# A graph network's convolutions as matmuls over a dense adjacency that is built first

## The chip, the cores and the metric

The program runs on one core of one Trainium2 chip. The metric is the device time of one execution in microseconds; lower is better. The kernel before took 4636.26 us (median of three runs, 4625.92 to 4641.4).

## What is computed

A graph has 3125 nodes with 256 features each and 103125 directed edges, sorted by their target. Two blocks follow one another: two graph convolutions (GCN), then two attention layers (GATv2). Each block adds its input and normalises every row. Only the first block is touched by the change, and one by-product of it that the second needs.

```python
def gcn_conv(x, src, dst, ew, W, b):          # twice, with a leaky ReLU (0.01) between
    h = x @ W                                 # 3125 x 256
    # self-loops of weight 1 are appended to src, dst and ew
    deg = segment_sum(ew, dst)                # per node
    dis = where(deg > 0, rsqrt(deg), 0)
    norm = dis[src] * ew * dis[dst]
    return segment_sum(h[src] * norm[:, None], dst) + b
x = layernorm(x + gcn_conv(leaky(gcn_conv(x, W1, b1)), W2, b2))
x = layernorm(x + gat2(elu(gat1(x))))         # 4 heads of 64, then 1 head of 256
```

## The kernel before

All tensors are fp32 but the transposed one-hots. The nodes are cut into 25 windows (`NWIN`) of 125 (`WN`). The edges, in the order of their targets, are cut into 806 tiles (`NT`) of 128; four tiles are a block (`NB` = 202 blocks). A block can reach over the border of two windows, so the work items are 228 pieces (`NG`), one for each pair of block and window, with tables that the kernel makes itself from the edge list (`codes`: block and window of each piece, read into registers).

The program is a row of stages, each its own block of instructions on all engines, with a barrier between: `consts`, `route` (edge list in, turned to edge-on-partition columns `dst_t`, `src_t`, `w_t`), `degrees` (the degrees, `dis`, and x @ W1 scaled by `dis` into `acc`, which it also stores to `table_d[0]`), `gcn_edges(0)`, `gcn_mid`, `gcn_edges(1)`, `gat_in(1)`, `gat_edges(1)`, `gat_in(2)`, `gat_edges(2)`, `finish`.

`gcn_edges(layer)` sums the weighted neighbours of one convolution. GpSimd gathers the source rows, one indirect DMA for each of the 806 tiles of 128 rows (`gather_blocks`, L1009), into a ring of 16 blocks `rows`. For each piece VectorE makes four weighted one-hots `selw` (L1146, 128 edges x 128 nodes), TensorE multiplies the four with the gathered rows (L1185, fp32, 256 columns) and VectorE adds the result to the window's rows of `acc` (L1157). In layer 0 the same loops also make what the attention layers need later: four bf16 one-hots `ohk` of each piece (L1164), turned by TensorE (L1193), copied from PSUM by ScalarE (L1215) and widened to fp32 (L1220), and stored from ScalarE's queue to `oh_d` and `ohT_d` (256 KB and 128 KB a piece). Some flags for the attention's segments (`marks`) are made at its start on VectorE.

`gcn_mid` applies bias, leaky ReLU and W2 window by window, and stores the rows to `table_d[1]`.

The attention stages use the same gather (806 indirect DMAs each), load the stored one-hots, and are not changed by the diff but for an index into the list of tables.

The order on each engine is the order of the code: `pipeline` unrolls 12 pieces, with a lag in pieces for each step, in a loop of 19 turns. Engines are bound by semaphores alone: GpSimd runs ahead in the ring until the pieces that free a slot are summed (`s_mm`), TensorE waits for a landed block (`s_landed`) and for its one-hots (`s_sel`).

Of the kernel before, what the change touches and what calls it, by code (L numbers as in the profile page):

```python
# [12 lines left out]
P = 128  # L13
N_NODES = 3125
N_EDGES = 103125
D = 256
# [30 lines left out]
META = 4  # L47
BIG = 1.0e30
# [147 lines left out]
def gnn_kernel(nc, a, out):  # L196
    ctx = ExitStack()
    with ctx:
# [18 lines left out]
        def close(st):  # L217
# [8 lines left out]
            with nc.Block() as block:  # L226
                @block.gpsimd
                def _(pool):
# [13 lines left out]
        table_d = [nc.dram_tensor(f"table{i}_d", (N_NODES, w), F32, kind="Internal").ap()  # L242
                   for i, w in enumerate((D, D, DX, DX))]
# [33 lines left out]
        natf_dst = sb("natf_dst", [P, NTJ, P], F32, marked)  # L277
        nat_w = sb("nat_w", [P, NTJ, P], F32, marked)
# [5 lines left out]
        same = sb("same", [P, NTJ, P], F32, marked)  # L284
        flg_all = sb("flg_all", [P, NTJ, 5, P], F32, marked)
        ends_all = sb("ends_all", [P, 2, NTJ], F32, marked)
        linesT = sb("linesT", [2 * NTJ, P], F32, marked)
        bidx = sb("bidx", [HG, 2], U32, marked)
        apart = sb("apart", [HG, 2, 2], F32, marked)
        link4 = sb("link4", [HG, 2, K], F32, marked)  # L290
        alone4 = sb("alone4", [HG, 2, K], F32, marked)
        into = sb("into", [NC, CH * K], F32, marked)
        alone_at = sb("alone_at", [NC, 2, CH * K], F32, marked)
        through = sb("through", [NC, 2, CH * K], F32, marked)
        carry_all = sb("carry_all", [NC, 4, CH * K], F32, marked)


        found = ExitStack()
        tri = sb("tri", [P, P], F32, found)
# [24 lines left out]
        def route():  # L324
# [5 lines left out]
            natf_src = sb("natf_src", [P, NTJ, P], F32, st)  # L330
# [315 lines left out]
        def one_hot(tile, w, b):  # L646

            return nc.vector.tensor_tensor(tile, nodes_of(w).unsqueeze(1).to_broadcast([P, K, P]),
                                           dst_t[:, bass.ds(b, 1), :].rearrange("p o k -> p (o k)").unsqueeze(2).to_broadcast([P, K, P]),
                                           ALU.is_equal)  # L650

        def degrees():
# [56 lines left out]
            s_W, s_mm, s_h, s_d, s_in, s_deg_all, s_root, s_dis, s_sc, s_set = (sem(n) for n in (  # L709
# [14 lines left out]
            with nc.Block() as block:  # L724
# [27 lines left out]
                def _(sp):  # L752
# [10 lines left out]
                    for v in range(TURNS):  # L763
                        if v == TURNS - 2:
                            sp.wait_ge(s_sc1, 1)
                        else:
                            sp.wait_ge(s_sc, v + 1 if v < TURNS - 2 else v)
# [141 lines left out]
                def _(act):  # L909
# [33 lines left out]
                    for v in range(*PARTS[0]):  # L943
                        scale(v, s_sc)
# [1440 lines left out]
```

## Time and profile before

| | us |
|---|---|
| median of 3 runs (range) | 4636.26 (4625.92 to 4641.4) |
| span of the profiled execution | 5635.5 |
| of it: `consts`, `route`, `degrees` | 0 to 104 |
| `gcn_edges(0)`, `gcn_mid`, `gcn_edges(1)` | 104 to 2552 |
| attention layer 1 (its edges 2690 to 4100) | 2552 to 4100 |
| attention layer 2 (its edges 4230 to 5570) | 4100 to 5570 |
| `finish` | 5570 to 5635.5 |

The profiled execution is 999 us longer than the median of the runs; no other time of it was taken, so its span stands for it. Times in rows below are from its start. An instruction's duration includes a fixed latency that the next one can overlap, so the spacing of starts is shorter than the mean duration. "Busy" is the union of such durations. An fp32 matmul stands in the trace as two TensorE instructions, each with its own weight load.

### The profile page before, as it was taken

The numbers are of one execution on the slowest core, as the hardware profiler recorded it, in microseconds if no ns is written. First come the engines' busy times: TensorE is split into PE (matmuls) and PEld (weight loads), VectorE is DVE, ScalarE is ACT, GpSimd is POOL, SyncE is SP. The second block draws the span as 40 slices with busy tenths as digits, with TensorE's granted clock in tenths as the row PEclk, the third lists the DMA queues.
The fourth block names the chain that finished last, engine by engine and source line by source line (L and its number), as shares of the span: only waits on it lengthen the run. The fifth ranks groups of instructions, "written<-read, shape, count | busy, mean of one in ns | idle before, by whom it ended". The sixth has DMA issues, their size and how long they took to land. (4 is left out here: it accounts for less than half of the span.)

```text
span 5635.5 us, 95010 instructions
## 1 busy us (share of the span) xinstructions
PE 3517.4 (62%) x15636; PEld 2585.4 (46%) x15637; DVE 3007.8 (53%) x9011; ACT 1856.5 (33%) x6057; POOL 3154.3 (56%) x3421
## 2 busy tenths in 40 slices
PE   4555555555555554556577676776755777777776
PEld 3344444444333333333455555555534555555554
DVE  5444444444322222225677777777765665665655
ACT  3222222122000000003476767666732333333334
POOL 4666666664666666661555555555325555555550
PEclk7777777777667777778788888888987888888887
DMA  4555555554323233334556556555535666665665
GB/s 138 159 168 160 162 159 167 156 167 125 89 87 91 87 90 89 89 89 104 149 172 172 171 168 177 172 170 165 148 83 150 176 171 168 175 172 168 179 172 136
DMA packets 469883, 816.01 MB, mean 145 GB/s; under 512 B 86378, under 2 KB 271484, under 8 KB 469692
## 3 DMA queue, kind: packets, MB, share of 16 engines
q0 software_dynamic: 156464, 429.23, 27.7%
q1 hardware_dynamic: 245866, 294.48, 17.6%
q10 hardware_dynamic: 67362, 90.53, 4.4%
q14 instruction: 167, 1.37, 0.1%
q8 instruction: 24, 0.39, 0.0%
HBM read 640.50 MB, written 173.40 MB: 144 GB/s over the span
## 5 line engine op out<-in xcount | busy, mean ns | idle before, releaser
L1009 POOL DMA_INDIRECT rows<-table_d,idx x3224 | 3068.0, 952 | 1981.3 <-issue 970.2
L1185 PE MATMUL psum<-rows,selw 128*128 x3648 | 1247.6, 499 | 1085.0 <-issue 416.1
L1185 PEld LDWEIGHTS psum<-rows,selw 128*128 128x128 f32 x3648 | 868.5, 251 | 1383.2 <-issue 1244.1
L2097 ACT ACTIVATE px<-rows,px 128x64 f32 (+1 forms) x4480 | 1280.6, 367 | 205.7 <-issue 140.5
L2162 PE MATMUL psum<-px,ohf 128*128 128x264 f32 (+1 forms) x3648 | 1141.4, 467 | 150.9 <-ACT px L2097 66.5
L1929 DVE TENSOR_TENSOR m<-rows,psum 128x1024 f32<-128x1024 f32 x456 | 554.3, 1216 | 878.3 <-remote 582.8
L2162 PEld LDWEIGHTS psum<-px,ohf 128*128 128x128 f32 x3648 | 801.7, 231 | 334.7 <-issue 99.4
L2113 PE MATMUL psum<-xr,ohT 125*128 x5472 | 780.5, 298 | 143.2 <-issue 54.8
L1157 DVE TENSOR_TENSOR acc<-acc,psum 125x256 f32 x456 | 189.7, 416 | 1239.3 <-DMA nat_w<-in_edge_weight_dram 431.2
L2113 PEld LDWEIGHTS psum<-xr,ohT 125*128 125x128 bf16 x5472 | 578.0, 107 | 336.2 <-issue 185.7
L1146 DVE TENSOR_SCALAR selw<-iotaw,dst_t,w_t 128x128 f32 x1824 | 528.8, 360 | 278.1 <-issue 273.0
L1653 ACT ACTIVATE root<-mv 125x5 f32<-125x5 f32 x5 | 1.1, 213 | 1217.6 <-DVE mv L1410 1217.6
L1215 ACT COPY ohTk<-psum 128x512 bf16<-128x512 bf16 x228 | 132.7, 582 | 641.5 <-remote 526.7
L2088 ACT COPY px<-pl 128x32 f32<-128x32 f32 (+1 forms) x456 | 100.2, 220 | 699.4 <-PE psum L2162 267.8
L1948 DVE SCALAR_TENSOR_TENSOR sc<-m,psum 128x256 f32<-128x256 f32 x912 | 324.2, 403 | 2.9 <-issue 2.8
L1957 DVE TENSOR_REDUCE lg<-sc 128x16 f32<-128x1024 f32 x228 | 278.1, 1220 | 10.3
L1941 DVE SCALAR_TENSOR_TENSOR sc<-m,psum 128x1024 f32<-128x1024 f32 x228 | 273.7, 1201 | 4.2 <-issue 4.1
L1220 ACT CAST ohfk<-ohk 128x512 f32<-128x512 bf16 x228 | 140.8, 618 | 318.6 <-issue 148.2
L1164 DVE TENSOR_SCALAR ohk<-iotaw,dst_t 128x128 bf16 x912 | 211.1, 309 | 21.4 <-issue 21.3
L2062 DVE SCALAR_TENSOR_TENSOR part<-part,keep_tab,psum 128x264 f32<-128x264 f32 (+1 forms) x380 | 180.2, 474 | 17.0 <-PE psum L2162 16.8
L2075 ACT ACTIVATE both<-both 96x128 f32<-96x128 f32 (+1 forms) x76 | 23.4, 308 | 424.7 <-DVE fac L2022 308.1
L2123 PE MATMUL psum<-ident,lg 128*96 128x128 f32 (+1 forms) x152 | 36.5, 328 | 134.4 <-issue 64.1
(321 smaller groups left out, 2052.9 us busy)
## 6 DMA issues: line engine op xcount, KB each, us to landing
ohf<-oh_d SPq DMA_DIRECT2D x456, 256.0 KB
oh_d<-ohfk ACTq DMA_DIRECT2D x228, 256.0 KB
ohT<-ohT_d SPq DMA_DIRECT2D x456, 128.0 KB
rows<-table_d,idx POOLq DMA_INDIRECT x3224
part_d<-part SPq DMA_DIRECT2D x228, 132.0 KB
part_d<-part SPq DMA_DIRECT2D x228, 129.0 KB
ohT_d<-ohTk ACTq DMA_DIRECT2D x228, 128.0 KB
flg<-flags_d SPq DMA_DIRECT2D x228, 40.0 KB
```

Source lines behind the costliest of these rows:

```text
L1009: pool.indirect_dma_start(out=rows[0:n, s % RING, k, :], out_offset=None, in_=table, in_offset=bass.IndirectOffsetOnAxis(ap=idx[0:n, s // ...
L1146: last = nc.vector.tensor_scalar(sel[:, g.pos % DEEP, k, :], nodes_of(w), dst_t[:, bass.ds(b, 1), k:k + 1].rearrange("p o k -> p (o k)"), ...
L1157: nc.vector.tensor_tensor(sums, sums, ps[g.pos % DEEP][0:WN], ALU.add).then_inc(s_acc, 1)
L1164: last = nc.vector.tensor_scalar(ohb[:, g.slot, k, :], nodes_of(w), dst_t[:, bass.ds(b, 1), k:k + 1].rearrange("p o k -> p (o k)"), None, ...
L1185: last = nc.tensor.matmul(ps[g.pos % DEEP], sel[:, g.pos % DEEP, k, :], rows[:, bass.ds(r, 1), k, :].squeeze(1), start=k == 0, stop=k == K ...
L1929: V.tensor_tensor(m[:, i], rows[:, bass.ds(r, 1), :, 0:D].squeeze(1), psX[i], ALU.add).then_inc(s_add, 1)
L1941: V.scalar_tensor_tensor(out=sc[:, i], in0=m[:, i], scalar=0.0, in1=psatt.unsqueeze(1).to_broadcast([P, K, D]), op0=ALU.max, op1=ALU.mult) ...
L1948: last = V.scalar_tensor_tensor(out=sc[:, i, k], in0=m[:, i, k], scalar=0.0, in1=psatt, op0=ALU.max, op1=ALU.mult, accum_out=lg[:, g.half, ...
L1957: V.tensor_reduce(out=kh(lg[:, g.half, g.place]), in_=sc[:, g.slot % 2].rearrange("p k (h c) -> p (k h) c", h=H), axis=AX.X, op=ALU.add).t ...
L2097: last = nc.scalar.activation(px[:, i, k, h, 0:C], rows[:, bass.ds(r, 1), k, h * C:(h + 1) * C].squeeze(1), ACT.Copy, scale=px[:, i, k, h, ...
L2113: last = nc.tensor.matmul(psX[i][:, k, :], ohT[0:WN, g.slot, k * P:(k + 1) * P], xr3[0:WN, bass.ds(w, 1), j, :].squeeze(1), start=j == 0, ...
L2162: last = nc.tensor.matmul(psA[i], ohf[:, g.pos % FS, k, :], px[:, i, k].rearrange("p h c -> p (h c)"), start=k == 0, stop=k == K - 1)
```

## The change

The three GCN stages go, and with them `table_d[0]`, the first table of gathered rows, and the stores to it at the end of `degrees`. In their place stand three stages.

`parts` works out, from the edge list in its natural layout (`natf_dst`, `natf_src`, `nat_w`: a tile of 128 edges on one partition), a second cut: targets in groups of 5 nodes (`GN`, 625 groups), and one part for each pair of tile and group that it touches, 1440 parts in all (`NP`, the rest empty). For each part it puts the tile's columns, rows and weights on partitions with one-hot matmuls (168 bf16 matmuls of 480 columns, L1206), exactly, as sums of two or three bf16 pieces: `col_at`, `row_at`, `w_at`. It also makes `slots` (a PSUM column for each part) and `units`.

`adjacency` builds, for each window of 125 targets, the dense matrix of edge weights against all 3125 sources. Each part is one fp32 matmul of 125 by 125 (L1329): the stationary operand `sw` is one-hot in the source's row in its window times the weight, the moving operand `where` is one-hot in (target in the group, source's window). The sum goes to a register-held column of PSUM, over what other parts have put there. 16 parts are a step, 90 steps. GpSimd makes ten of a step's `where` one by one (L1281), VectorE the other six in one instruction (L1258) and all 16 `sw` (L1294). ScalarE copies finished units of PSUM (20 targets by 25 source windows, 500 columns) to a strip and zeroes them. SP stores each of the 25 strips (125 x 3125 fp32) to `adj_d`.

`convolve` runs both layers: 50 products, one for each layer and window, each 25 fp32 matmuls of 256 columns (L1630) with the strip (`adj_w`, three in flight) stationary and the feature rows moving. The self-loop, bias, ReLU and W2 of a finished window run beside the next one. The 228 pieces' one-hots for the attention layers, and the flags, are made in the same loops, five pieces to a product, and are now stored from SP's queue. No row is gathered before the attention layers. In the diff below the loops of `adjacency` are those of GpSimd, VectorE, ScalarE and TensorE in this order, those of `convolve` are SP's and TensorE's.

```diff
-            rows = sb("rows", [P, RING, K, D], F32, st)
-            sel = sb("selw", [P, DEEP, K, P], F32, st)
-                    gather_blocks(pool, table_d[layer], idx, rows, s_idx, s_rows, s_mm, s_landed, s_mm, 6)
-                        for k in range(K):
-                            last = nc.tensor.matmul(ps[g.pos % DEEP], sel[:, g.pos % DEEP, k, :], rows[:, bass.ds(r, 1), k, :].squeeze(1),
-                                                    start=k == 0, stop=k == K - 1)
...
+        def parts():
...
+                    for j in range(NTJ):
+                        if j >= 2:
+                            dve.wait_ge(s_tiles, j - 1)
+                        link(V.tensor_scalar(tmp[j % 2][:], iotaw[:, 0:NP], begin[:, j:j + 1], None, ALU.is_ge))
+                        V.scalar_tensor_tensor(out=of_tile[:, j], in0=iotaw[:, 0:NP], scalar=end[:, j:j + 1], in1=tmp[j % 2][:],
+                                               op0=ALU.is_lt, op1=ALU.mult).then_inc(s_tiles, 1)
...
+                    gather((0, 1, 2), (offb[:, 0], offb[:, 1]), s_heads)
+                    gather((3, 4, 5), (colb[0], colb[1]), s_atcol)
+                    gather((6, 7, 0), (srb,), s_atrow)
+                    gather((1, 2, 3), (wb[0], wb[1], wb[2]), s_atw)
...
+        def adjacency():
...
+                    for s in range(NS):
+                        if s >= DEEP:
+                            pool.wait_ge(s_mm, STEP * (s - DEEP + 1))
+                        for i in range(POOLED):
+                            p = s * STEP + i
+                            last = nc.gpsimd.tensor_scalar(where[:, s % DEEP, i, :], aim[:], col_at[:, p:p + 1], None, ALU.is_equal)
...
+                        place(s, POOLED, STEP).then_inc(s_where, 1)
+                        for i in range(STEP):
+                            last = V.tensor_scalar(sw[:, s % DEEP, i, :], iota[:, 0:WN + 1], row_at[:, p:p + 1], w_at[:, p:p + 1],
+                                                   ALU.is_equal, ALU.mult)
...
+                            nc.scalar.copy(strip[0:WN, w % 2, :, nodes_at(i)],
+                                           sums_of(u).rearrange("p (d s) -> p s d", s=NWIN)).then_inc(s_strip, 1)
+                            nc.scalar.copy(sums_of(u), zero[0:WN, 0:sums_of(u).shape[1]]).then_inc(s_free, 1)
...
+                        for i in range(STEP):
+                            nc.tensor.matmul(flat[0:WN, bass.ds(at_slot[i], MC)], sw[:, g.slot, i, 0:WN], where[:, g.slot, i, :],
+                                             start=False, stop=True, skip_group_check=True).then_inc(s_mm, 1)
...
+        def convolve():
...
+                    for n in range(CONVS):
+                        for k in pieces_in(n):
+                            store(k)
+                        if n + RA < CONVS:
+                            load(n + RA)
...
+                        for s in range(NWIN):
+                            last = nc.tensor.matmul(psC[n % 2], adj_w[0:WN, n % RA, s, :], rows[0:WN, s, 0:D],
+                                                    start=s == 0, stop=s == NWIN - 1)
+                            if s % PER == PER - 1 and s // PER < len(ks):
+                                turn(ks[s // PER])
+                            if s == 8 and 0 < n <= NWIN:
+                                turn_rows(n - 1)
+                            if s == 18 and 0 < n <= NWIN:
+                                weigh(n - 1)
```

On TensorE, a turn of the loop of `gcn_edges(0)` in the kernel before reads (one piece; `selw` are the weighted one-hots, `rows` the gathered rows, `ohk` the one-hots for the attention):

```order
L192 ISA
L1185 REGISTER_ALU
L1185 ISA
L1185 MATMUL psum<-rows,selw 128x256
L1185 ISA
L1185 MATMUL psum<-rows,selw 128x256
L1185 ISA
L1185 MATMUL psum<-rows,selw 128x256
L1185 ISA
L1185 MATMUL psum<-rows,selw 128x256
L1193 MATMUL psum<-identb,ohk 128x128 x4
```

Each piece had a wait for its landed block (L192) and four products with gathered rows. In the changed kernel the same engine, inside one product of `convolve`, reads (`adj_w` is a strip of the adjacency, `acc` the feature rows, `aT` the turned rows of the window before):

```order
L1630 MATMUL psum<-acc,adj_w 125x256 x5
L1588 MATMUL psum<-identb,ohk 128x128 x4
L1630 MATMUL psum<-acc,adj_w 125x256 x4
L1596 MATMUL psum<-ident,act_in 128x125 x2
L1630 MATMUL psum<-acc,adj_w 125x256
L1588 MATMUL psum<-identb,ohk 128x128 x4
L1630 MATMUL psum<-acc,adj_w 125x256 x5
```

The products now come in fives with nothing between that a gather has to release. On VectorE the loop of `adjacency` reads (two steps of 16 parts):

```order
L1258 TENSOR_TENSOR where<-aim,col_at 128x750 [waits adj_summed]
L1294 TENSOR_SCALAR sw<-iota,row_at,w_at 128x126 x16
L1258 TENSOR_TENSOR where<-aim,col_at 128x750 [waits adj_summed]
L1294 TENSOR_SCALAR sw<-iota,row_at,w_at 128x126 x16
```

and on GpSimd beside it:

```order
L1281 TENSOR_SCALAR where<-aim,col_at 128x125 [waits adj_summed]
L1281 TENSOR_SCALAR where<-aim,col_at 128x125 x9
L1281 TENSOR_SCALAR where<-aim,col_at 128x125 [waits adj_summed]
L1281 TENSOR_SCALAR where<-aim,col_at 128x125 x9
```

Both engines work on the same step at the same time, with addresses that are fixed in the code.

## Rows read from the trace of the kernel before

**Rows 1.** The page: busy us of each engine (share) and instructions.
```profile
PE 3517.4 (62%) x15636; PEld 2585.4 (46%) x15637; DVE 3007.8 (53%) x9011; ACT 1856.5 (33%) x6057; POOL 3154.3 (56%) x3421
```

**Rows 2.** Windows by stage: us, busy of PE, PEld, DVE, ACT, POOL, PEclk, DMA share, GB/s.
```profile
104.00:1350.00 1246.00, 723.73 (x2889) 538.85 (x2890) 555.08 (x2123) 277.95 (x502) 787.65 (x842) 0.75 0.52 161
1362.00:2552.00 1190.00, 608.45 (x1824) 436.54 (x1824) 342.21 (x1140) 0.00 (x0) 771.67 (x830) 0.73 0.31 90
2690.00:4100.00 1410.00, 982.37 (x5047) 736.36 (x5044) 1039.24 (x1868) 957.95 (x3910) 743.54 (x804) 0.85 0.58 166
4230.00:5570.00 1340.00, 983.98 (x5056) 739.32 (x5056) 807.15 (x3220) 449.04 (x1254) 746.88 (x806) 0.83 0.60 168
```

**Rows 3.** Timeline of GpSimd in the second convolution: start, us, what.
```profile
1802.54 0.95 POOL L1009 DMA_INDIRECT rows<-table_d,idx  x1 [0.30 <-issue]
1804.80 0.94 POOL L1009 DMA_INDIRECT rows<-table_d,idx  x1 [1.32 <-issue]
```

**Rows 4.** GpSimd's waits, 1362 to 2552: us in total, times, longest.
```profile
POOL rows L1009 <- issue: 288.9, 768, 4.2
POOL rows L1009 <- DMA nat_w<-in_edge_weight_dram: 100.9, 29, 6.3
```

**Rows 5.** GpSimd's waits in the first attention layer, 2690 to 4100.
```profile
POOL rows L1009 <- remote: 197.0, 80, 3.4
POOL rows L1009 <- issue: 196.7, 631, 1.0
POOL rows L1009 <- PE psum L2113: 187.3, 57, 8.4
```

**Rows 6.** TensorE's timeline: start, us, an fp32 matmul of 256 columns.
```profile
5606.42 1.06 PE L2238 MATMUL psum<-own_rows,with_row 125*125 125x256 f32 x2
5607.28 0.91 PE L2236 MATMUL psum<-x1s,with_row 126*125 126x256 f32 x2
...
5609.33 0.60 PE L2236 MATMUL psum<-x1s,with_row 126*125 126x256 f32 x2
5609.76 0.60 PE L2238 MATMUL psum<-own_rows,with_row 125*125 125x256 f32 x2
```

**Rows 7.** TensorE's timeline, first attention input: fp32 matmuls of four columns.
```profile
2602.96 0.50 PE L1764 MATMUL psum<-watt,yT 128*125 128x4 f32 x4
```

**Rows 8.** Windows as in rows 2: a dense fp32 stretch of that stage.
```profile
2580.00:2600.00 20.00, 18.62 (x77) 10.41 (x75) 9.27 (x19) 14.36 (x39) 0.00 (x0) 1.00 0.23 65
```

**Rows 9.** The weighted one-hots on VectorE: durations in ns, min/median/max.
```profile
L1146 DVE TENSOR_SCALAR selw<-iotaw,dst_t,w_t x1824: 327/341/603, 114.6 to 2545.1; 128x128 f32 x183
```

**Rows 10.** Timeline of VectorE and GpSimd in `degrees`.
```profile
25.53 0.22 DVE L879 COPY from_first<-ident 128x128 f32<-128x128 f32 x1
25.66 0.22 DVE L880 COPY from_last<-ident 128x128 f32<-128x128 f32 x1
...
76.35 2.74 POOL L748 IOTA iotaw<- 128x3128 f32 x1
76.57 0.17 DVE L864 SCALAR_TENSOR_TENSOR deg<-deg,deg_last 128x15 f32<-128x15 f32 x1
76.78 2.34 DVE L865 TENSOR_SCALAR degpos<-deg 128x15 f32<-128x15 f32 x1
```

**Rows 11.** Groups of instructions, 0 to 100: busy us, mean ns, idle before.
```profile
L884 DVE TENSOR_TENSOR is_last<-dst_t,psum 128x808 f32<-128x808 f32 x1 | 1.0, 997 | 0.1
L730 POOL TENSOR_TENSOR w_other<-other,nat_w 128x896 f32<-128x896 f32 x1 | 2.1, 2113 | 1.6 <-DVE other L881 1.6
```

**Rows 12.** TensorE turns one piece's bf16 one-hots, in layer 0's timeline.
```profile
607.91 0.39 PE L1193 MATMUL psum<-identb,ohk 128*128 128x128 bf16 x4
```

**Rows 13.** A group of the page, on ScalarE, busy us and mean ns.
```profile
L1220 ACT CAST ohfk<-ohk 128x512 f32<-128x512 bf16 x228 | 140.8, 618 | 318.6 <-issue 148.2
```

**Rows 14.** Windows as in rows 2: loads of 2.5 KB rows, loads of 1 KB rows.
```profile
38.00:40.00 2.00, 2.00 (x4) 0.84 (x3) 1.92 (x8) 0.16 (x2) 1.55 (x2) 0.50 1.02 385
...
2556.00:2560.00 4.00, 0.00 (x0) 0.00 (x0) 1.17 (x1) 0.00 (x0) 0.00 (x0) 0.55 1.08 190
```

More of the change, by code:

```diff
@@ L47 @@
 META = 4
+GN = 5
+GROUPS_ALL = N_NODES // GN
+STEP = 16
+NS = -(-(NT + GROUPS_ALL) // (3 * STEP)) * 3
+NP = NS * STEP
+THIRD = NP // 3
+BANKS = 8
+UG = 4
+WG = WN // GN
+UW = -(-WG // UG)
+UNITS = NWIN * UW
+MC = GN * NWIN
+POOLED = 10
+CENTRE = 89375
+CONVS = 2 * NWIN
+RA = 3
+OSL = 6
+PER = 5
 BIG = 1.0e30
@@ new lines, in parts @@
+            colb = [sb("colb", [P, NTJ, P], BF16, st) for _ in range(2)]
+            col_r = sb("col_r", [P, NTJ, P], F32, st)
+            wb = [sb("wb", [P, NTJ, P], BF16, st) for _ in range(3)]
+            w_r = [sb("w_r", [P, NTJ, P], F32, st) for _ in range(2)]
+            tmp = [sb("from_begin", [P, NP], BF16, st) for _ in range(2)]
+            of_tile = sb("of_tile", [P, NTJ, NP], BF16, st)
+            below = sb("below_unit", [P, 3, THIRD], BF16, st)
+            limit = sb("limit", [P, 2], F32, st)
@@ L1070, in gcn_edges @@
             LINES = 16 * 7
+            AHEAD = 2
+            pieces_in = lambda n: range(min(n * PER, NG), min((n + 1) * PER, NG))
+            window_in = lambda n: n % NWIN
             with nc.Block() as block:
@@ new lines, in _ @@
+                    for n in range(RA):
+                        load(n)
+                    sp.dma_start(W[:, :, 0:D], a["L0_gnn_W2"].rearrange("(h p) d -> p h d", p=P)).then_inc(s_W, 16)
+                    bcast_row(sp, b, a["L0_gnn_b1"], s_W)
+                    line = lambda v: v.rearrange("(o e) -> o e", o=1)
+                    sp.dma_start(link_d[0:1, 0:1], none[:, 0:1]).then_inc(s_lines, 16)
+                    sp.dma_start(line(in_line(link_d)[TILES + 1:TILES + K]), none[:, 0:K - 1]).then_inc(s_lines, 16)
@@ L1107, in _ @@
                     DVE = mybir.EngineType.DVE
+                    V = nc.vector
                     def marks():
[L1110 removed]
                         done = [0]
@@ L2350, in gnn_kernel @@
         degrees()
-        gcn_edges(0)
-        gcn_mid()
-        gcn_edges(1)
+        adj = ExitStack()
+        col_at, row_at, w_at = (sb(n, [P, NP], F32, adj) for n in ("col_at", "row_at", "w_at"))
+        slots = sb("slots", [1, NP], I32, adj)
+        units = sb("units", [1, NS], I32, adj)
+        unit_ends = sb("unit_ends", [1, UNITS], I32, adj)
+        parts()
+        adjacency()
+        adj.close()
+        convolve()
         marked.close()
```

712 lines of the change are left out of this document (466 added, 246 removed).

## The prediction

> **What bounds the kernel now.** I read the page's totals first, then the windows by stage, then one engine's waits in each. The totals [rows 1] show no engine over 62% of the span, so the bound has to be sought stage by stage. In both convolutions [rows 2] GpSimd is the busiest engine after TensorE (788 of 1246 us, 772 of 1190), and TensorE's busy time stands at a mean granted clock of 0.75 and 0.73, a mix of its two levels, which tells of bursts and pauses. GpSimd's timeline shows that its pauses are not free time: an indirect DMA of 0.95 us is followed by 0.30 us in which nothing is waited for, and each fourth by 1.32 us [rows 3]. Over the second convolution it waits 289 us for "issue", and 101 us for the largest other release [rows 4]. So the gather's own instructions pace the convolutions: 806 of them in 1190 us, 1.48 us each, of which 1.25 is the instruction and its issue. In the attention stages GpSimd waits 397 us of 1410 for others [rows 5], VectorE is busy for 1039 and TensorE for 982 [rows 2]: there the gather is one of several limits.
>
> **Profile and runs.** The sum is made against the profiled execution, span 5635.5 us; the runs' median is 4636.26, 999 us less. That gap has to be put somewhere. TensorE's rows double exactly when its clock halves (below), so they hold nothing that the profiler adds; I put it into the indirect DMAs, of which there are 4 x 806 = 3224. If they cost x less each in an unprofiled run, the two convolutions (bound by them) win 1612x, the attention layers a part a of 1612x. With a = 1, x is 0.31 us and the attention's part 500 us; with a = 0.4, 285 us. As GpSimd waited for others 397 of 1410 us, I take a = 0.6: x = 0.39 us, 375 us in attention and 624 in the convolutions. So in a run the convolutions of the kernel before take about 2448 - 624 = 1824 us. The attention stages stay as they are, and keep their 375.
>
> **The change, part by part**, in profiled time. The three stages that go stand from 104 to 2552.
>
> *`degrees`*: its last vector work ends at 96, the table's stores land by 104 and go. About -6 us; it ends at 98.
>
> *`parts`*, new: VectorE makes `of_tile` in 7 pairs of 1440 columns. By the 808-column row of 997 ns [rows 11], 1.2 ns a column, a two-input one takes 1.7 us and the one-input one 1.0 at its double rate: 19 us. Ten 896-column operations are some 11 us, thirty small links at 0.2 us 6, the chain on `group` 14. The 168 matmuls of 480 columns take 0.2 us at the full clock and 0.4 at the half: 34 to 67 us, of which the first half waits for `of_tile`. On the path: 32 before the matmuls, then some 48 of them and copies. 80 us (65 to 110).
>
> *`adjacency`*, new, 90 steps of 16 parts, each engine three steps deep, so the slowest engine of a step sets it.
> - VectorE: an `sw` is like `selw`, median 341 ns [rows 9]. Two copies of 220 ns started 130 ns apart [rows 10], so the spacing is 90 ns under the duration: 0.25 us. 16 x 0.25 = 4.0; the 750-column `where` 0.85 to 0.9, by its columns [rows 11]. 4.9 us.
> - TensorE: an fp32 matmul of 256 columns at full clock takes 0.434 us (5609.76 less 5609.33), at the half clock 0.86 (5607.28 less 5606.42), with new weights for each and the load hidden [rows 6]. 125 columns are half of that, 0.21. Loads alone, four with 4-column matmuls in 0.50 us, are 0.1 us apart [rows 7], the same as half a matmul of 125 columns, so a load can just hide. 16 x 0.21 = 3.4 us; with nothing hidden, or at the half clock, 6.7.
> - GpSimd: no one-input row of that size. Its iota wrote 3128 columns in 2.74 us, 0.875 ns each [rows 10]; its two-input product took 2.36 ns a column [rows 11]. For 125 columns that is 0.11 to 0.30 us, plus a start. Ten are 2 to 4 us: hidden behind VectorE by themselves.
> - The two together: while the iota ran, VectorE's two-input operation took 0.17 us, but its one-input TENSOR_SCALAR of 15 columns took 2.34 us and ended with the iota [rows 10]. `sw` is such a one-input TENSOR_SCALAR, and GpSimd now runs beside all of them. Low end: nothing is held, 4.9 us. High end: all is in line, 4.9 + 3.0 = 7.9. I take the part of each GpSimd operation in which it moves its columns as held, 10 x 0.11 = 1.1: 6.0 us. That is nearest to the iota's row, whose whole length was columns.
>
> The Trainium skill ("GPSIMD Engine Reference", 1. Specifications) says that GpSimd's SBUF interfaces are shared with VectorE, and that they contend with a two-port mode or with two SBUF inputs. The trace agrees for the first (2.34 us) and not for the second (0.17 us, with two inputs). By the rule `where` on VectorE would be held too, which with all in line is the 7.9 us again, not more.
>
> ScalarE has 175 units of a copy and a zeroing, 0.6 us each [rows 13], with a register load and a wait between: some 2.2 us of the 3.1 that a unit lasts. Hidden; its cover ends under 4.3 us a step. SP's strips, 25 of 1.56 MB, are 5 us each at 350 GB/s [rows 14], once in 21 us. Hidden but for the last, with the last unit 15 us. 90 x 6.0 + 15 + 5 at the start = 560 us (460 to 730).
>
> *`convolve`*, new. On TensorE 1250 + 50 fp32 matmuls of 256 columns x 0.434 = 564; 228 turns of four, four in 0.39 us of which some 0.2 is latency that the next one overlaps [rows 12]; between that and 0.39, near the low end, 0.24 each, 55 (89 at the high); 50 turned blocks of feature rows 12: 631 us, and 18 for joins between kinds. The stretch at 2580 to 2600 shows the clock at 1.00 with TensorE busy 18.6 of 20 us in fp32 [rows 8]; here it is as dense, so full clock. VectorE: 912 `ohk` at 0.25 at most, by `selw`, 228 us, and 40 for the windows' ends. ScalarE: 456 copies at 0.6 [rows 13], 270. Both hidden. What waits on the path: the start, where the first matmul waits for the first strips and then for W2 queued behind three of them, 4.7 MB at 350 GB/s, 14 us and latencies, while the flags are made: 18. The end 3. In all 670 us (640 to 780).
>
> *Transfers*: 50 strips are 78 MB and the one-hots' stores 90 MB, 168 MB in 670 us, 251 GB/s. The trace has 385 GB/s at a share of 1.02 with 2.5 KB runs and 190 at 1.08 with 1 KB runs [rows 14]; the strips have 12.5 KB runs, the stores 2 and 1 KB. At 350 for strips and 2 KB and 190 for 1 KB: 223 + 171 + 158 = 552 us. Hidden, with little to spare.
>
> *Sum*: 98 + 80 + 560 + 670, and 5 for the barriers, is 1413 where 2552 stood: the span falls by 1139 to 4496. The attention's 375 us less in a run: 4121. From the other side, 4636 - 1824 + (1413 - 104) = 4121. I say 4120.
>
> **The rivals.**
> - *VectorE and GpSimd in line.* The 2.34 us row speaks for it, the short hold of a 125-column operation against. 90 x 1.9 = 171 more: 4290.
> - *Transfers bound `convolve`.* If all 168 MB go at the 190 GB/s of 1 KB runs, it takes 883 us, 213 more: 4330. For it: stores and loads mixed never passed 180 GB/s in a long stretch, 161 to 168 [rows 2]. Against: there the share was 0.52 to 0.60.
> - *Better than I think.* Steps at 4.9 us (-99) and the attention's part of the gap 500 us (-125): 3896, say 3900. For it: GpSimd's columns cost little; a could be 1.
> - *Slower: TensorE stays at the half clock.* Place: `convolve` and `adjacency`, which TensorE carries. At 1.2 GHz the fp32 matmuls cost 0.86 us, `convolve` +580 us, a step at least 6.7, +75, `parts` +30: 4805. It decides from +516 us on, that is when `convolve` runs below about 0.6 of full clock. For it: 0.73 to 0.75 in the convolutions now [rows 2]. Against: those have pauses, and rows 8 is dense and at 1.00.
>
> **Chances.** Forecast 0.50, better 0.18, in line 0.15, transfers 0.12, slower 0.05. The range takes in the bounds of both doubtful terms, the hold and the gap: 3880 to 4340. A difference under 0.3% (14 us) can't be told from none. Faster 0.95, same 0.01, slower 0.04 (in a fifth of the half-clock cases it falls short of +516).
>
> **What would show it.** Right: no DMA_INDIRECT before the attention but `degrees`' 25 and the flags' four; a span near 4500 that is some 375 above the run's time; L1329 in groups of 16 every 6 us; L1630 at 0.434 us start to start at a granted clock near 1. Hold: L1294 longer than 341 ns while L1281 runs. Wrong: L1630 waiting for `adj_w`'s DMA (transfers), a clock near 0.5, L1329 in one dense row (then TensorE sets the step, not VectorE), or a gap between span and run that stays at 999 or vanishes, which would put it elsewhere than into the gathers.

## The result and the profile after

The changed kernel takes 3845.48 us (median of 4 runs, 3841.91 to 3846.22), the kernel before 4634.13 (median of 4, 4625.92 to 4641.4): a ratio of 0.830, 95% interval 0.829 to 0.831. The profiled execution took 3845.3 us with a span of 3843.6, so the gap of 999 us between span and runs that stood in front of the prediction is gone. The prediction said 4120 (3880 to 4340): the direction was right and the new stages together came out as forecast; the total was 275 us too high, and the measured time lies 35 us under the range. Of the times below, one run of experiment 2 (4519 us at a granted clock of 0.78, where its other three took 4416 to 4435 at 0.86) was in a slow state and is left out of its ratio.

The page, as in [rows 1]:

```profile
PE 2980.3 (78%) x17564; PEld 2375.2 (62%) x17565; DVE 2904.3 (76%) x8382; ACT 2023.3 (53%) x6416; POOL 2197.2 (57%) x2660
```

The windows by stage, with the columns of [rows 2]: `parts`, `adjacency`, `convolve`, then a stretch in each attention layer and everything behind the convolutions.

```profile
98.00:154.00 56.00, 36.90 (x172) 17.04 (x172) 42.89 (x40) 6.53 (x7) 0.30 (x1) 0.81 0.00 0
154.00:766.00 612.00, 400.04 (x2909) 380.82 (x2909) 501.58 (x1545) 189.35 (x350) 583.16 (x904) 0.88 0.29 69
781.00:1414.00 633.00, 632.11 (x3562) 536.15 (x3562) 245.62 (x1018) 267.95 (x506) 8.93 (x10) 1.00 0.92 262
1560.00:2560.00 1000.00, 789.18 (x4764) 610.23 (x4762) 961.41 (x1743) 890.25 (x3713) 742.88 (x794) 0.98 0.78 225
...
2700.00:3760.00 1060.00, 855.62 (x5072) 658.92 (x5072) 824.92 (x3257) 450.18 (x1245) 773.05 (x837) 0.93 0.78 216
...
1414.00:3843.60 2429.60, 1866.66 (x10764) 1411.79 (x10764) 2045.21 (x5564) 1513.88 (x5450) 1570.39 (x1682) 0.93 0.73 204
```

GpSimd is now the full engine in `adjacency` (583 of 612 us), TensorE in `convolve` (632 of 633, at a clock of 1.00). The convolutions end at 1413, where the prediction's sum says 1413. The attention, which the diff does not touch, went through 794 GpSimd instructions (nearly all gathers) in 1000 us where [rows 2] has 804 in 1410, at 225 GB/s in place of 166. That is where the missing 275 us lie.

The lines that carry the new stages: durations in ns as min/median/max, then first and last start.

```profile
L1281 POOL TENSOR_SCALAR where<-aim,col_at x900: 590/597/1382, 154.5 to 736.4; 128x125 f32<-128x125 f32 x180
L1258 DVE TENSOR_TENSOR where<-aim,col_at x90: 924/940/1164, 154.5 to 723.6; 128x750 f32<-128x750 f32 x90
L1294 DVE TENSOR_SCALAR sw<-iota,row_at,w_at x1440: 331/337/441, 155.3 to 728.7; 128x126 f32<-128x126 f32 x180
L1329 PE MATMUL psum<-where,sw x2880: 270/272/569, 162.1 to 740.8; 128*125 128x125 f32 x192
L1630 PE MATMUL psum<-acc,adj_w x1250: 377/379/792, 781.0 to 1112.9; 125*125 125x256 f32 x179
L1630 PE MATMUL psum<-second,adj_w x1250: 377/379/433, 1113.3 to 1412.7; 125*125 125x256 f32 x179
```

Two steps on VectorE and part of one on GpSimd, from the timeline (start, us, what, how many, and in brackets the idle time before):

```profile
409.75 1.16 DVE L1258 TENSOR_TENSOR where<-aim,col_at 128x750 f32<-128x750 f32 x1 [3.91 <-PE psum L1329]
410.83 4.68 DVE L1294 TENSOR_SCALAR sw<-iota,row_at,w_at 128x126 f32<-128x126 f32 x16
415.44 0.92 DVE L1258 TENSOR_TENSOR where<-aim,col_at 128x750 f32<-128x750 f32 x1
416.29 4.62 DVE L1294 TENSOR_SCALAR sw<-iota,row_at,w_at 128x126 f32<-128x126 f32 x16
420.83 0.93 DVE L1258 TENSOR_TENSOR where<-aim,col_at 128x750 f32<-128x750 f32 x1
```

```profile
405.72 4.06 POOL L1281 TENSOR_SCALAR where<-aim,col_at 128x125 f32<-128x125 f32 x7
```

VectorE needs 5.39 us for a step (415.44 to 420.83) and after some steps waits (3.91 us before 409.75); GpSimd never waits: 900 in 582 us, 6.47 us for ten. Seven that stand alone in the second timeline start 0.58 us apart ((4.06 less 0.596) / 6). The one that starts with VectorE's `where` at 400.3 is the odd one, and those while VectorE has nothing at all to do (406 to 409.7) are like the rest:

```profile
L1281 POOL TENSOR_SCALAR where<-aim,col_at x1: 1363/1363/1363, 400.3 to 400.3; 128x125 f32<-128x125 f32 x1
...
L1281 POOL TENSOR_SCALAR where<-aim,col_at x7: 593/596/597, 405.7 to 409.2; 128x125 f32<-128x125 f32 x7
```

So ten cost 10 x 0.58, and 0.7 for the one that VectorE's two-input instruction holds. The Trainium skill ("GPSIMD Engine Reference", 1. Specifications) says that GpSimd's interfaces to SBUF are shared with VectorE, and contend with it in a two-port mode or with two SBUF inputs. For two inputs the trace agrees: 1363 ns beside the two-input `where`, 0.59 us beside the one-input `sw`. Which mode `sw` runs in no trace shows.

VectorE is held too, though the median of 337 ns hides it. The group's mean on the page is 364 ns, and in a stretch of the changed kernel with GpSimd busy throughout, ten `sw` have a median of 365 and a maximum of 404:

```profile
L1294 DVE TENSOR_SCALAR sw<-iota,row_at,w_at 128x126 f32<-128x126 f32 x1440 | 417.9, 364 | 0.0
...
L1294 DVE TENSOR_SCALAR sw<-iota,row_at,w_at x10: 334/365/404, 278.6 to 281.3; 128x126 f32<-128x126 f32 x10
```

The last step of experiment 3 (below) has 16 `sw` with GpSimd done. They take 4.17 us together, where the same 16 take 4.62 to 4.68 in the timeline above:

```profile
732.25 0.94 DVE L1258 TENSOR_TENSOR where<-aim,col_at 128x750 f32<-128x750 f32 x1 [0.58 <-POOL where L1281]
733.11 4.17 DVE L1295 TENSOR_SCALAR sw<-iota,row_at,w_at 128x126 f32<-128x126 f32 x16
```

Start to start that is 0.256 us alone (all 30 such pairs of that run lie at 0.255 to 0.257) and 0.287 in the mean beside GpSimd (1350 pairs of the changed kernel). In the stretch of the ten they alternate: an `sw` that starts some 40 ns after a GpSimd instruction takes 400 ns, the next one 335. A step's 16 `sw` are so held for 0.4 to 0.5 us.

### The profile page after: what moved, and what is told of

Same layout as the page of the kernel before. It is cut to its first block and busy times, and to the rows that moved or that the text cites. A ratio compares the mean times of both kernels' runs of the same rounds, so it can differ in the third digit from the quotient of the medians.

```text
span 3843.6 us, 88662 instructions
## 1 busy us (share of the span) xinstructions
PE 2980.3 (78%) x17564; PEld 2375.2 (62%) x17565; DVE 2904.3 (76%) x8382; ACT 2023.3 (53%) x6416; POOL 2197.2 (57%) x2660
## 5 line engine op out<-in xcount | busy, mean ns | idle before, releaser
L997 POOL DMA_INDIRECT rows<-table_d,idx x1612 | 1538.6, 954 | 507.4 <-issue 450.5
L2468 PE MATMUL psum<-px,ohf 128*128 128x264 f32 (+1 forms) x3648 | 952.1, 406 | 67.0 <-ACT px L2403 61.0
L2468 PEld LDWEIGHTS psum<-px,ohf 128*128 128x128 f32 x3648 | 680.3, 197 | 203.9 <-issue 45.9
L1281 POOL TENSOR_SCALAR where<-aim,col_at 128x125 f32<-128x125 f32 x900 | 582.5, 666 | 0.1
L1329 PE MATMUL psum<-where,sw 128*125 128x125 f32 x2880 | 390.0, 302 | 189.4 <-POOL where L1281 153.5
L1329 PEld LDWEIGHTS psum<-where,sw 128*125 128x125 f32 x2880 | 375.3, 215 | 204.8 <-issue 204.8
L1294 DVE TENSOR_SCALAR sw<-iota,row_at,w_at 128x126 f32<-128x126 f32 x1440 | 417.9, 364 | 0.0
L1630 PE MATMUL psum<-acc,adj_w 125*125 125x256 f32 x1250 | 306.6, 386 | 25.7 <-DMA b_in<-in_L_gnn_b_dram 25.7
L1630 PE MATMUL psum<-second,adj_w 125*125 125x256 f32 x1250 | 292.6, 383 | 0.0
L1630 PEld LDWEIGHTS psum<-acc,adj_w 125*125 125x125 f32 x1250 | 224.0, 189 | 53.4 <-DMA b_in<-in_L_gnn_b_dram 26.0
```

The source lines that it names most:

```text
L997: pool.indirect_dma_start(out=rows[0:n, s % RING, k, :], out_offset=None, in_=table, in_offset=bass.IndirectOffsetOnAxis(ap=idx[0:n, s // ...
L1281: last = nc.gpsimd.tensor_scalar(where[:, s % DEEP, i, :], aim[:], col_at[:, p:p + 1], None, ALU.is_equal)
L1294: last = V.tensor_scalar(sw[:, s % DEEP, i, :], iota[:, 0:WN + 1], row_at[:, p:p + 1], w_at[:, p:p + 1], ALU.is_equal, ALU.mult)
L1329: nc.tensor.matmul(flat[0:WN, bass.ds(at_slot[i], MC)], sw[:, g.slot, i, 0:WN], where[:, g.slot, i, :], start=False, stop=True, skip_group ...
L1630: last = nc.tensor.matmul(psC[n % 2], adj_w[0:WN, n % RA, s, :], rows[0:WN, s, 0:D], start=s == 0, stop=s == NWIN - 1)
L2468: last = nc.tensor.matmul(psA[i], ohf[:, g.pos % FS, k, :], px[:, i, k].rearrange("p h c -> p (h c)"), start=k == 0, stop=k == K - 1)
```

## The experiments

They form five groups, each on one chip with the kernel before beside it. In the group of experiments 9 to 11 the chip was as quick as the one of the result above (before: 4623.3 us for 4634.13; that it is the same chip is not on record), in the other four slower (before: 5630.78, 5675.18, 5640.1 and 5634.05 us). The slow groups ran on three different chips, experiments 12 to 14 and 15 to 17 on the same one. I call this a difference between chips, as the runs of an unedited kernel in a group lie within 0.5% or so, and the chip used twice was slow twice; each other chip was used by one group only. Times are compared within a group; stages between groups.

**1. The kernel before once more.** No edit.

> The kernel before, unchanged, profiled once more. My theory of the prediction (each indirect DMA costs 0.31 to 0.39 us more under the profiler): the span is again near 5635 us, 999 above the runs, with 3083 us from the start of the attention to the end. Rival (that one execution was slow by itself and the profiler adds nothing): the span is within some 5 us of the runs' 4634; the attention and the finish take 2430 us, as they do in the profile of the changed kernel (3843.6 less 1414), so the three convolution stages take about 2100; the gather runs at about 1.25 us an indirect DMA, with few waits for others.

5634.08 us for the profiled run, span 5631.9, and nine unprofiled runs beside it of 5616 to 5642. The profiler adds nothing; every run on this chip is slow. So neither "the profiler makes indirect DMAs dearer" nor any other reading in which span and run differ can stand. The span of 5635.5 that the prediction started from fits a true run of a slow chip.

**2. Eight one-hots of a step on GpSimd instead of ten.**

```diff
-POOLED = 10
+POOLED = 8
```

> In the adjacency stage GpSimd makes 8 of a step's 16 where tiles in place of 10, VectorE 8 in place of 6. Theory now: GpSimd sets the step (0.645 us for each of ten tiles, 6.45 us; VectorE needs 5.5 and waits). Then GpSimd needs 5.2 us, VectorE 5.5 + 0.26 = 5.8, which becomes the bound: 90 x 0.65 = 58 us less, 3787 us. Rival (prediction: VectorE's one-hots, held by GpSimd, set the step): VectorE gets 0.26 us more a step, 23 us slower, 3868. Second rival (the two are in line): what GpSimd loses, VectorE gains, within 15 us of 3845.

4433.83 us, ratio 0.788 (0.786 to 0.790), against 0.799 (0.798 to 0.800) of the unchanged kernel in experiment 5. 720 GpSimd instructions in 507 us in place of 900 in 582, and no waiting left on either engine:

```profile
L1281 POOL TENSOR_SCALAR where<-aim,col_at x720: 588/595/1633, 164.0 to 670.8; 128x125 f32<-128x125 f32 x180
...
L1258 DVE TENSOR_TENSOR where<-aim,col_at x90: 1182/1187/1201, 164.0 to 665.8; 128x1000 f32<-128x1000 f32 x90
```

GpSimd set the step at 6.47 us, as fewer of its instructions shorten it. With eight the step is 5.64. GpSimd was expected at 5.2 and isn't: its first instruction of each step now takes 1.63 us beside the 1.19 us `where`, the other seven 0.58 each, 5.65 together. Both engines are busy without a break, so which of them sets the 5.64 is not shown.

**3. VectorE's `where` behind GpSimd's ten.**

```diff
+                        dve.wait_ge(s_wherep, s + 1)
                         place(s, POOLED, STEP).then_inc(s_where, 1)
```

> VectorE waits for GpSimd's ten where tiles of the step before it makes its own part, so that while VectorE works GpSimd is at the next step only when it may be, and the two overlap less. Theory (GpSimd's 597 ns for a tile of 125 columns is its own price, not made by VectorE beside it): the L1281 spacing stays near 0.645 us where the two still overlap and is nearly that where they don't; the step stays GpSimd's 6.45 us or a little more, total within 60 us of 3845. Rival (the shared port makes the 597 ns): tiles made while VectorE waits take clearly less, 0.3 to 0.4 us, and L1294 falls from 0.29 us of spacing to 0.25.

4503.92 us in one run. The 900 took 568 us; each is still 594 ns in the median, and the longest 1305. The edit does not part the two for good, since GpSimd starts its next ten while `where` runs. That 0.59 us is GpSimd's own price shows in the row of seven above, with VectorE idle; this run has 34 more such instructions, at a median of 593. Its time can be set only beside experiment 16's 4502 us on another slow chip.

**4. W2 ahead of the second and third block of the adjacency.**

```diff
-                    for n in range(RA):
-                        load(n)
+                    load(0)
                     sp.dma_start(W[:, :, 0:D], a["L0_gnn_W2"] ...)
                     bcast_row(sp, b, a["L0_gnn_b1"], s_W)
+                    for n in range(1, RA):
+                        load(n)
```

> At the start of the convolve stage SP issues W2 and the bias behind the first strip of the adjacency and not behind the third. Theory: TensorE waited 25.7 us there for the bias's DMA, of which the flags on VectorE need 10; it starts about 15 us sooner and nothing else waits: 3830 us. Rival (the transfers are the limit of the stage, DMA share 0.92 to 0.99): what is gained at the start is lost by waits for strips 1 and 2, under 5 us of gain, 3842.

4489.82 us, ratio 0.797 (0.795 to 0.799). The first product starts 28.9 us after GpSimd's last `where` (748.5 to 777.4) in place of 44.6 (736.4 to 781.0) in the result's trace: 16 us. So 16 us of the idle time before the products were the queue; TensorE still waits 10 us for the bias's DMA there, for 26 without the edit.

**5 to 8, on a slow chip.** The changed kernel; edits 2 and 4 together; and both kernels with gathers that read rows 0 to 127 only:

```diff
-                nc.gpsimd.tensor_copy(idx[:, half], src_t[:, bass.ds(chunk * CHUNK, CHUNK), :]).then_inc(s_idx[half], 1)
+                nc.gpsimd.iota(idx[:, half], pattern=[[0, CHUNK], [0, K]], base=0, channel_multiplier=1).then_inc(s_idx[half], 1)
```

> The changed kernel itself, beside the kernel before, on whatever chip this call gets. If the slow chip is slow only in stages that gather rows, the changed kernel takes about 4500 us where the kernel before takes 5631 (ratio 0.80), with the adjacency's last product near 750 us and the convolutions' last near 1414 us as where it took 3845; the whole difference between the chips (655 us) lies behind 1414 us, in the attention. If the slow chip is slow in everything, the stages before 1414 us are 17% longer too (near 1650 us). Should the chip be the quick one (kernel before 4634), it takes 3845 again.

> Eight instead of ten one-hots a step on GpSimd, and the second weight's load ahead of the second and third adjacency blocks. If GpSimd's 0.645 us each sets the adjacency's step (6.45 us of 90 steps), then 8 leave VectorE the bound at 8 x 1000/8 columns in one instruction of 1.19 us and 16 x 0.285 us, 5.75 us a step: 63 us less than the unchanged one in this call, and about 10 to 15 us more for the products that start earlier: 70 to 78 us less together. Rival: the two don't add up, since the transfers into the first block set the start of the products whatever the order; then 63 us.

> The changed kernel, but every gather of the attention reads rows 0 to 127 of the table (left out: the real source rows; same instructions, packets and bytes). If scattered addresses are what the slow chip is slow at, the attention takes its 2430 us of the quick chip or less and the run 3850 us. If it is the GpSimd-written descriptors, or the queues, whatever the address, nothing changes: 4500 us on the slow chip (3845 on the quick one).

> The kernel before, but all its gathers read rows 0 to 127 of their tables (left out: the real source rows). If scattered addresses cost the slow chip its 999 us, this takes 4630 us or less there. If not, 5631 us. On the quick chip: 4634 us if addresses don't matter, less if they do.

Before 5675.18 us; the changed kernel 4532.43, ratio 0.799 (0.798 to 0.800); with both edits 4432.73, ratio 0.782 (0.780 to 0.783); same rows 4526.79 and, of the kernel before, 5673.62. Addresses cost nothing. Both edits together save 100 us; their stages show 74 (582 to 508 us) and 17 (45.4 to 28.1). The changed kernel's own stages are the same as on the quick chip up to the convolutions' end (1429 for 1413, 13 of the 16 us before `adjacency`, with no pause there and no cause found), and behind it the slow chip takes 3100 us for 2430:

```profile
L1630 PE MATMUL psum<-second,adj_w x1250: 377/379/433, 1129.4 to 1428.8; 125*125 125x256 f32 x179
...
1560.00:2560.00 1000.00, 682.35 (x3544) 511.84 (x3545) 735.24 (x1306) 662.72 (x2704) 560.15 (x600) 0.86 0.59 167
```

What differs there? Not the gather (a median of 951 and 952 ns), not its packets (a median of 161 ns on both), not the matmuls of the convolutions (379 ns on both). It is the register instructions of the engines' own queues. The same two of SyncE's lines and one of ScalarE's in the attention, the quick chip, then the slow one:

```profile
L2187 SPq FUSED_REGOPS  x408: 37/37/46, 1611.3 to 3727.3; - x136
L2187 SPq MOVE part_d<-part x408: 29/29/29, 1611.4 to 3727.3; - x136
L2403 ACTq FUSED_REGOPS  x4480: 46/46/57, 1567.5 to 3772.6; - x195
```

```profile
L2187 SPq FUSED_REGOPS  x408: 3/37/737, 1666.5 to 4413.5; - x136
L2187 SPq MOVE part_d<-part x408: 2/29/729, 1666.6 to 4413.6; - x136
L2403 ACTq FUSED_REGOPS  x4480: 4/46/1396, 1612.8 to 4458.8; - x195
```

An instruction of 29 ns now and then takes 729. And the sign was there in the profile that the prediction was made from, in the same lines of the kernel before:

```profile
L1881 SPq FUSED_REGOPS  x408: 3/37/729, 2792.7 to 5519.3; - x136
L1881 SPq MOVE part_d<-part x408: 3/29/732, 2792.7 to 5519.4; - x136
```

I counted such pauses in the traces: register and branch instructions of SyncE, ScalarE, VectorE and GpSimd of over 0.3 us, those that end within 60 ns of each other (on two or three engines at once) as one, with the longest of them as its length. The table leaves TensorE out.

```
kernel, chip                    in the graph convolutions    behind them
before, slow (first profile)    622, 437 us                  991, 680 us
before, slow, again (exp. 12)   630, 441 us                  965, 662 us
changed, slow (exp. 5)          0                            1052, 734 us
same rows, slow (exp. 7)        0                            1044, 731 us
changed, quick                  0                            0
```

TensorE's register instructions pause too, mostly in the graph convolutions of the kernel before. With them its first profile has 817 pauses of 576 us there and 994 of 685 us behind; a row of them, which never passes 42 ns in the products of `adjacency` on the quick chip:

```profile
L1185 PEldq FUSED_REGOPS  x1824: 3/46/1403, 115.8 to 2547.2; - x183
```

**9 to 11, on the quick chip.** One gather in four, the rest of the rows left at zero; 304 more gathers beside the convolutions; and every one-hot turned twice.

```diff
-                    for k in range(K):
+                    for k in range(1):
```
```diff
+                    for i in range(EXTRA):
+                        if i % 8 == 0 and i:
+                            pool.wait_ge(s_extra, 16 * i)
+                        pool.indirect_dma_start(out=extra[:, i % 8, :], ..., in_=link_d, ...).then_inc(s_extra, 16)
```
```diff
-                        for i in range(K):
+                        for i in (*range(K), *range(K)):
```

> The changed kernel with one gather in four in the attention (left out: three of four, whose rows stay zero). On the slow chip, register instructions of SyncE, ScalarE, VectorE and GpSimd that take 0.03 to 0.05 us now and then take 0.70 to 0.73 us in the attention, and never on the quick chip. If the gathers bring these pauses, a quarter of the gathers brings about a quarter of them, and the run falls from 4532 us to 3500 to 3900 us. If it is the loops themselves (the attention is the only stage looped on these engines) and the gathers are innocent, the pauses stay as dense and the run stays over 4300 us.

> The changed kernel with 304 more gathers, of 16 bytes a partition, by GpSimd beside the convolutions, where nothing waits for them; the convolutions are written out, with no loop, and VectorE has register instructions there (one block's one-hots each). If gathers bring the pauses on the slow chip, register instructions of VectorE of 0.045 us take up to 0.73 us between 900 and 1400 us, where there were none, and the run is 0 to 30 us longer. If pauses belong to loops, none appear there and the time is the same within 0.3%.

> The changed kernel with each of the 912 one-hots turned twice in the convolutions (the second over the first, same result). TensorE was busy for all of the 633 us and the DMA engines for 0.90 to 0.94 of them. If TensorE bounds the stage, 912 more turns of some 0.08 to 0.10 us cost 70 to 90 us. If the transfers do (the rival of the prediction), at most 20 us.

Before 4623.3 us. One gather in four: 3705.53, so on the quick chip three quarters of the gathers cost 140 us. Extra gathers: 3960.24; beside the strips' transfers they ran on past the stage's end, so the time tells nothing of the stage itself. Neither says anything on pauses, for the four traces of quick chips have none. Turned twice: 3894.92, ratio 0.843 (0.841 to 0.844); the products' two passes end 52 us later (782.5 to 1466.3 for 781.0 to 1412.7), 0.057 us for each of the 912. That is under the 0.08 expected and far over the transfers' 20: TensorE bounds the stage.

**12 to 14, on a slow chip** (before 5640.1 us): the kernel before profiled, the quarter of the gathers again, and 200 extra gathers.

> The kernel before, unchanged. On the quick chip its profile has no pause and its span is 4620 to 4640 us; with the attention and the finish at the 2430 us that the changed kernel takes for them there, the last product of the graph convolutions ends near 2200 us (2552 us in the slow profile), so the 999 us part as 350 for the graph convolutions and 650 for the attention. If the forecast's split were right (624 and 375), it ends near 1928 us. On a slow chip: 5630 to 5680 us and nothing new.

> The changed kernel with one gather in four in the attention (left out: the other three, whose rows stay zero); on the quick chip this took 3705.5 us, 130 to 140 us less than the unchanged one. On a slow chip: if the gathers bring the pauses, there are about a quarter as many and the run takes 3750 to 3950 us; if the loops do, they stay as dense and it takes over 4250 us.

> The changed kernel with 200 more gathers by GpSimd beside the convolutions, a stage with no loop on any engine (with 304 of them they reached past its end and cost the quick chip 115 us). On a slow chip: if gathers bring the pauses, VectorE's register instructions there (0.045 us) take up to 0.73 us between 900 and 1350 us, where there were none; if loops do, none appear. Its time: within 30 us of the unchanged one on the same chip.

5629.77, 3714.42 and 4520.13 us. With a quarter of the gathers the slow chip is 9 us slower than the quick one, and behind the convolutions not at all (2287 and 2288 us); with all of them the same chip is 657 us slower (experiment 16). 16 pauses are left, all SyncE's, of experiment 16's 957, and the same window stands at the quick chip's values, the granted clock included:

```profile
1560.00:2560.00 1000.00, 787.18 (x4777) 609.73 (x4776) 971.59 (x1761) 885.87 (x3695) 188.48 (x215) 0.98 0.52 148
```

The loops and their register instructions are all still there, so the pauses come with the gathers. They fall much faster than the gathers' number: a quarter was expected to bring a quarter of the pauses and 3750 to 3950 us. The extra gathers make the test the other way round: VectorE's register instructions beside the convolutions, where experiments 5 and 16 have none over 132 ns, now reach 690, 9 pauses in all. First experiment 5, then this one:

```profile
L1507 DVEq FUSED_REGOPS  x782: 57/57/132, 880.0 to 1375.2; - x196
```

```profile
L1515 DVEq FUSED_REGOPS  x777: 2/57/690, 880.0 to 1378.6; - x195
```

Nine are few only because VectorE is the one engine with many register instructions in that stage. They are 9 of its 1045 there (0.9%), and in the attention of the same run, with gathers of whole rows, 38 of 4451 (0.9%). So gathers bring the pauses, and on VectorE those of 16 bytes at about the rate of those of 1 KB, as far as nine can tell. The 200 came at 44 in 100 us, the attention's come at some 58 on a slow chip, and a quarter of them at 19 brings almost none. What between 19 and 44 makes the difference stays open.

**15 to 17, on the chip of 12 to 14** (before 5634.05 us): the kernel before profiled, the changed kernel, and edits 2 and 4 together.

> As before for the kernel before: on a quick chip a span of 4620 to 4640 us with no pause in it, the graph convolutions' end near 2200 us and the attention behind it near 2430 us; by the prediction's split the end near 1928 us and the attention 2708 us. On a slow chip 5630 to 5680 us.

> The changed kernel unchanged: 3845 us on a quick chip, 4532 us on a slow one.

> Eight one-hots a step on GpSimd and W2 ahead of the second and third block: on a slow chip these were 100 us less than the changed kernel, of which its stages show 74 for the steps and 17 for the start. Neither stage has pauses, so a quick chip should show 85 to 100 us less too: 3745 to 3760 us. If part of it was the attention's own scatter on the slow chips, 91 us.

5639.39 us; 4502.18, ratio 0.798 (0.795 to 0.801); 4412.10, ratio 0.782 (0.780 to 0.784). The two edits save 90 us here and 100 in experiment 6, around the 91 that the stages show. This version beats both kernels in both groups; it has no run on a quick chip. As its two stages show no pauses anywhere, I estimate 3845 less 91 there, about 3755 us. Six, seven or nine one-hots on GpSimd were not tried: with fewer, VectorE, already full at eight, gets more; with nine I estimate 9 x 0.58 and a hold between the 0.7 us found with ten and the 1.03 with eight, 6.1 us a step on GpSimd.

## Why the prediction was right, and where it failed

| | predicted us | measured us |
|---|---|---|
| `degrees` and `parts`, to the start of `adjacency` | 178 | 154 |
| `adjacency` to its last product | 545 | 586 |
| last unit, barrier, store, first blocks and W2 | 38 | 40 |
| `convolve` from its first product | 652 | 632 |
| to the convolutions' end | 1413 | 1413 |
| all behind it, in a run | 2708 | 2430 |

The convolutions' end at 1413 is hit by luck as far as it is exact: the parts are off by -24, +41, +2 and -20 us, and these cancel.

*The step that failed* is "I put it into the indirect DMAs", together with the split 624 to 375: a dearer gather that isn't there, and 375 us for the attention's part of the gap where 653 were measured, which is the 275 us by which the total is off. By experiment 1 the profiler adds nothing, so the first profile, with the span and the pauses of a slow chip, and the first runs, with a quick one's time, most likely came from different chips; which they were is not on record. Taking the slow chip's 999 us away, the attention loses 653 (3083 in the first profile, 2430 now), not 375; the graph convolutions of the kernel before keep 346 of the 999, so they and the start take 4634 - 2430 = 2204 us in a quick run, not 1824 + 104. I had reasoned from which engine bounds a stage: GpSimd paces the convolutions, so they should feel a dearer gather in full. But the gather is not dearer: a median of 951 and 952 ns on a slow and a quick chip. What takes time are pauses in the register instructions of all five engines. Why they cost the attention most is only argued: its loops have such instructions on SyncE and ScalarE at each piece, ahead of loads and products. The pauses' own number doesn't give the split: without TensorE's they part as 437 to 680 us (39 to 61%), with them as 576 to 685 (46 to 54%), and the loss as 346 to 653 (35 to 65%). That the attention of the kernel before takes 2430 us in a quick run is derived from its being the same code, and from its equal time on one slow chip, 3073 us in the changed kernel (experiment 16) and 3078 and 3080 in the kernel before (experiments 12 and 15, from the last product); there is no profile of the kernel before on a quick chip.

*The change is thus worth two different sums*: 789 us on the quick chip, and 1132 to 1143 on the slower chips (experiments 16 and 5), since the stages that it takes away have pauses and the new ones have none. The span forecast of 4496 was for a slow chip, and it took 4502 to 4532 us there.

*`adjacency`*: right in sum (6.0 us a step forecast, 6.47 found, within 460 to 730), wrong in its parts. VectorE was to be the bound at 4.9, held by GpSimd for 1.1. Its own price was right: 0.85 for `where` and 16 x 0.256 for `sw`, 4.95 us. The hold was there but under half as long as forecast, 0.44 us, which gives the 5.39 found. But VectorE was not the bound. GpSimd was sized at 2 to 4 us from an iota's and a product's row, and took 6.47: 4.6 ns a column (0.58 us for 125) where those rows have 0.875 and 2.36. The 0.30 us there was no upper end, as neither row was of its form. And there was a second hold, the other way: GpSimd waits on VectorE's two-input instruction, 0.7 us a step. The prediction weighed that pair only as a hold of VectorE, and had nothing for it on GpSimd.

*`convolve`*: right, TensorE's 632 us against 631, at the full clock. The joins' 18 us didn't come. *Transfers*: hidden, as forecast, 262 GB/s at a share of 0.92, over the 161 to 168 of [rows 2]; experiment 11 excludes them as the bound. *Slower rival*: clock 0.88 in `adjacency`, 1.00 in `convolve`; excluded. *Better rival*: its mechanism for the steps (4.9) fell, that for the attention's share (500 us) was in the right direction and too small; that its 3900 comes so near is luck. *`parts`*: 56 us from 98, for 80: TensorE's 168 matmuls took 37 us busy at 0.81.

Two readings in the prediction are wrong and change nothing in its sum: in both convolutions GpSimd was busier than TensorE (788 for 724 us, 772 for 608 in [rows 2]), not second to it, and a step of 6.7 us is 63 us over the forecast's 6.0, not 75.

## What to carry to other kernels

If a profile's span and the runs disagree by 20%, first find out whether they come from the same chip, and read the minimum and the maximum of the cheapest queue instructions (a register move of 29 ns that once takes 732) before any share is given to a stage by reasoning. Size an instruction by a row of the same engine and the same form; a bound from another form of it is none. Look at an instruction's mean beside its median before calling it unheld: the 337 ns of `sw` hid a mean of 364. On some chips dense gathers by GpSimd's queue cost far more than their own 1.25 us each, in every loop beside them, and a dense matmul that takes their place is worth more there (1132 to 1143 us for 789).

## What was unexpected of the hardware

- On the slow chips the register instructions of all five engines (TensorE's mostly in the graph convolutions of the kernel before) paused for about 0.70 us at a time, at times two or three engines at the same moment, while GpSimd issued dense gathers: in experiment 5 1052 pauses, 734 us, and 670 us lost behind the convolutions. In the four traces of quick chips there was not one. With a quarter of the gathers 16 were left, and 200 gathers of 16 bytes brought them where there were none. What in the chip pauses them stays open; so does why a quarter of the gathers brings so much less than a quarter of the pauses.
- A GpSimd fp32 compare of 128x125 with a scalar for each partition takes 0.58 us start to start whether VectorE runs one-input instructions or nothing, and 1.36 us when a two-input VectorE instruction of 750 columns starts with it (1.63 with one of 1000). In return VectorE's one-input instruction of 126 columns starts every 0.287 us beside such compares and every 0.256 alone.
- fp32 matmuls of 125 x 125 x 125 with new weights each ran at 0.235 us (the 32 instructions of a step in 3.75 us, from 162.12 in the changed kernel), their loads beside them.
